# A five-layer graph network on one core: counts written tile by tile, x normalized by ScalarE, and the last neighbour sum with adjacency blocks stationary

## What is computed

```python
h = maximum(layernorm(x), 0)
# first network: encoder, five layers with shared GRU weights, decoder
h = maximum(h @ enc_w1.T + enc_b1, 0) @ enc_w2.T + enc_b2
for w in conv_w:                                  # 5 layers
    agg = segment_sum((h @ w)[src], dst)
    h = gru(agg, h)                               # gates r, z, n; wih, whh
h = maximum(h, 0)
x = x + sigmoid(maximum(h @ dec_w1.T + dec_b1, 0) @ dec_w2.T + dec_b2)
# second network: two sums with a normalized adjacency
h = maximum(layernorm(x), 0)
v = dinv[src] * dinv[dst]                         # dinv = degree ** -0.5, from src, loops added once more
h = relu(spmm(v, h) @ W1.T + b1)                  # 256 hidden features
x = x + spmm(v, h) @ W2.T + b2
```

## Time and profile before

| | before |
|---|---|
| median of 3 runs | 767.2 us (766.75 to 767.5) |
| the profiled execution | 767.26 us, span 765.5 us |
| mean granted clock of TensorE | 0.998 of full speed |
| busy TensorE / VectorE / ScalarE / GpSimd | 95% / 43% / 43% / 5% |
| chain that ended last | TensorE 83%, VectorE 10%, ScalarE 3% |

### The profile page before, as it was taken

The page is one execution under the profiler, slowest core; times in us unless marked ns, Lnnn a source line. Parts: engine busy times, 40 slices in busy tenths (PEclk is TensorE's granted clock), DMA queues, the critical chain, the costliest instruction groups (busy, mean ns, idle before and its releaser), DMA issues.

```text
span 765.5 us, 9328 instructions
## 1 busy us (share of the span) xinstructions
PE 726.1 (95%) x3792; PEld 370.4 (48%) x3792; DVE 331.5 (43%) x666; ACT 329.4 (43%) x452; POOL 40.2 (5%) x55
## 2 busy tenths in 40 slices
PE   2678999999999999999999999999999999999997
PEld 2545666544444445444454444544445545555443
DVE  7999998442412225122250322645654731123102
ACT  2687988653643336343363433523446411112000
POOL 5110000000000000000000000120000410000000
PEclk9999999999999999999999999999999999999999
DMA  6000020441501214013140032430001100000001
GB/s 181 5 1 2 1 73 2 77 96 37 97 0 36 48 36 88 1 21 62 36 88 1 14 69 37 79 93 2 1 0 64 39 1 1 2 1 2 23 20 46
DMA packets 78699, 28.38 MB, mean 37 GB/s; under 512 B 70245, under 2 KB 77798, under 8 KB 78523
## 3 DMA queue, kind: packets, MB, share of 16 engines
q1 hardware_dynamic: 77690, 26.93, 16.4%
q0 software_dynamic: 240, 0.66, 0.3%
q10 hardware_dynamic: 720, 0.13, 0.1%
HBM read 8.03 MB, written 2.60 MB: 14 GB/s over the span
## 4 chain that ended last, share of the span: by engine, by line
PE 83%; DVE 10%; ACT 3%; DMA 1%; issue 1%; POOL 1%; SPq 1%; DVEq 0%; ACTq 0%
PE PSA L1173 36%; PE PSA L1328 13%; PE PSA L1252 5%; DVE CT L816 4%; PE PSA L1185 3%; PE PSA L1194 3%; PE PSA L1187 3%; PE PSA L1189 3%; PE PSA L1193 3%; PE PSA L1196 3%; PE PSA L1116 3%; PE PSA L1316 2%; ACT AT L1486 1%; PE PSA L1304 1%; DVE stat L781 1%
## 5 line engine op out<-in xcount | busy, mean ns | idle before, releaser
L1173 PE MATMUL PSA<-AT,H 128*128 128x512 fp8e3 (+1 forms) x1522 | 287.0, 348 | 0.6 <-DMA H<-H 0.6
L1173 PEld LDWEIGHTS PSA<-AT,H 128*128 128x128 f16 x1522 | 131.6, 98 | 158.2 <-issue 13.6
L1009 DVE SCALAR_TENSOR_TENSOR rS<-PSA,bias,rS 128x512 f32<-128x512 f32 (+1 forms) x35 | 23.9, 682 | 270.6 <-ACT rS L1537 270.6
L1537 ACT ACTIVATE rS<-PSA,bias 128x512 f32<-128x512 f32 (+1 forms) x35 | 22.1, 632 | 203.7 <-PE PSA L1193 203.7
L1486 ACT ACTIVATE AT<-PSA 128x1000 fp8e3<-128x1000 f32 (+1 forms) x79 | 92.0, 1231 | 25.1 <-PE PSA L1116 24.8
L816 DVE TENSOR_TENSOR CT<-CT 128x2048 bf16<-128x2048 bf16 x80 | 92.2, 1204 | 3.0 <-PE PSA L1116 3.0
L1460 ACT ACTIVATE CTL<-AT 128x3125 fp8e3<-128x3125 fp8e3 (+1 forms) x25 | 69.9, 2797 | 0.0
L1116 PE MATMUL PSA<-CT 128*128 128x125 bf16 x625 | 48.5, 232 | 20.5 <-DVE CT L816 16.9
L1328 PE MATMUL PSA<-CT,H 128*128 128x512 fp8e3 (+1 forms) x336 | 65.5, 351 | 1.2 <-POOL H L726 1.2
L1328 PE MATMUL PSA<-CT,AT 128*128 128x512 fp8e3 (+1 forms) x336 | 65.0, 351 | 0.0
L1116 PEld LDWEIGHTS PSA<-CT 128*128 128x128 bf16 x625 | 42.2, 103 | 34.3 <-DVE CT L816 24.0
(11 more groups left out here) (166 smaller groups left out, 644.8 us busy)
## 6 DMA issues: line engine op xcount, KB each, us to landing
AT<-scale_scratch SPq DMA_DIRECT2D x1, 1562.5 KB, 6.4
H<-in_x SPq DMA_DIRECT2D x1, 1536.0 KB
out<-AT SPq DMA_DIRECT2D x6, 256.0 KB
comb_scratch<-CT SPq DMA_DIRECT2D x1, 960.0 KB, 4.2
comb<-comb_scratch SPq DMA_DIRECT2D x5, 192.0 KB, 3.1
H<-yS SPq DMA_TRANSPOSE x48, 2.5
H<-in_x SPq DMA_DIRECT2D x1, 512.0 KB, 5.0
CT<-AT SPq DMA_TRANSPOSE x25, 3.9
```

The source lines that it names most:

```text
L1173: last = nc.tensor.matmul(bank[:, 0:w], H16[:, l % 2, t, h, :], AT3[:, t, n0:n0 + w], start=(t == 0 and h == 0), stop=(t == T - 1 and (h = ...
```

## The change

Three parts.

First, ScalarE's eviction of a group of counts goes over tiles outside and windows inside: for each tile it writes 8 x 5 = 40 neighbouring bytes, and reads five counts from each of eight windows. Before, it went over windows outside: for each window and tile it wrote 5 bytes.

Second, VectorE no longer normalizes: it computes -mean x scale for a chunk (`shifts`, one instruction of four elements), and ScalarE does `Relu(scale * x + shift)` tile by tile, after the evictions of an odd batch. VectorE's eviction of the transposed chunk becomes a plain copy.

Third, in the second sum the block of counts from 128 sources to 128 destinations is stationary, and the two halves of Z16 of that source tile, 256 columns, move. A tile u of 128 destinations is a chain of 24 such matmuls and one of 128 columns with ZP (`tile_sum`, `tile_ends`), and its bank has nodes on partitions, the high halves' sum in columns 0 to 127 and the low halves' in 128 to 255. No transposes follow: VectorE adds the two halves, scaled, to x in two chained instructions. Five banks (TILES) rotate. The last two tiles (53 nodes) are summed and turned as before. SP stores two tiles at a time.

```diff
-        SUM1, SUM2 = (1, 0, 6), (0, 7, 1)
+        SUM1, TILES = (1, 0, 6), (0, 7, 4, 1, 6)
+        STARTED = len(TILES)
@@ SyncE
-            for c in range(NC):
-                sp.wait_ge(output_ready, c + 1)
...
+            for g in range(FG):
+                if g == FG // 2:
+                    sp.wait_ge(last_output_ready, 1)
+                    for (p0, p1), us, (n0, n1) in node_pairs(NC - 1):
+                        stored(p0, p1, us, n0, n1)
+                sp.wait_ge(output_ready, 2 * g + 2)
+                stored(0, P, (2 * g, 2 * g + 2), 2 * P * g, 2 * P * (g + 1))
@@ VectorE
-            def normalized(s):
+            def shifts(s):
 
                 t0, nt = CH[s]
                 dve.wait_ge(roots_ready, s + 1)
-                for t in range(t0, t0 + nt):
-                    k = rows(t)
-                    last = nc.vector.tensor_scalar(X32[0:k, t, :], X32[0:k, t, :], mv[0:k, t, 0:1], lnsc[0:k, t:t + 1],
-                                                   ALU.subtract, ALU.mult)
-                last.then_inc(tile_normalized, 1)
+                nc.vector.scalar_tensor_tensor(lnb[:, t0:t0 + nt], mv[:, t0:t0 + nt, 0], -1.0, lnsc[:, t0:t0 + nt],
+                                               ALU.mult, ALU.mult).then_inc(shifts_ready, 1)
...
-                nc.vector.tensor_scalar(aggS[:, 0:w], PS[EA][:, 0:w], 0.0, None, ALU.max).then_inc(x_copied, 1)
+                nc.vector.tensor_copy(aggS[:, 0:w], PS[EA][:, 0:w]).then_inc(x_copied, 1)
...
-                for c, (t0, nt) in enumerate(CU):
-                    dve.wait_ge(sum2_transposed, c + 1)
...
+                for u in range(2 * FG):
+                    bank = PS[TILES[u % STARTED]]
+                    dve.wait_ge(sum2_ready, u + 1)
+                    link(nc.vector.scalar_tensor_tensor(OUT[:, u, :], bank[:, 0:F], dinvO[:, u:u + 1], X32[:, u, :],
+                                                        ALU.mult, ALU.add))
+                    nc.vector.scalar_tensor_tensor(OUT[:, u, :], bank[:, F:2 * F], dinvO[:, u:u + 1], OUT[:, u, :],
+                                                   ALU.mult, ALU.add).then_inc(output_ready, 1)
@@ TensorE
+            def tile_sum(u, s0, s1):
+
+                for s in range(s0, s1):
+                    nc.tensor.matmul(PS[TILES[u % STARTED]][:, 0:2 * F], CT2[:, s // 2, nodes(u), s % 2],
+                                     Z16[:, s, :, :].rearrange("p h f -> p (h f)"), start=(s == 0), stop=False)
+
+            def tile_ends(u):
+
+                nc.tensor.matmul(PS[TILES[u % STARTED]][:, 0:F], CTL[:, nodes(u)], ZP[:, :], start=False, stop=True
+                                 ).then_inc(sum2_ready, 1)
...
+            for u in range(STARTED, 2 * FG):
+                pe.wait_ge(output_ready, u - STARTED + 1)
+                tile_sum(u, 0, 24)
+                tile_ends(u)
@@ ScalarE
-                        AT3[0:P, :, w0 * W:(w0 + gw) * W].rearrange("p t (w d) -> p w t d", w=gw),
-                        counts[:, 0:gw, 0:W * T].rearrange("p w (t d) -> p w t d", t=T),
+                        AT3[0:P, :, w0 * W:(w0 + gw) * W].rearrange("p t (w d) -> p t w d", w=gw),
+                        counts[:, 0:gw, 0:W * T].rearrange("p w (t d) -> p t w d", t=T),
...
+            def normalized(s):
+
+                t0, nt = CH[s]
+                act.wait_ge(shifts_ready, s + 1)
+                for t in range(t0, t0 + nt):
+                    k = rows(t)
+                    last = nc.scalar.activation(X32[0:k, t, :], X32[0:k, t, :], ACT.Relu, bias=lnb[0:k, t:t + 1],
+                                                scale=lnsc[0:k, t:t + 1])
+                last.then_inc(tile_normalized, 1)
...
             for b in range(NBT):
                 windows(b)
+                if b % 2 == 1 and b // 2 < NC:
+                    normalized(b // 2)
```

More of the change, by code:

```diff
@@ L635, in _, with stored @@
             packed(ZP, Z16, projected_packed)
-            for c in range(NC):
-                sp.wait_ge(output_ready, c + 1)
[L638 to L645, removed]
+            def stored(p0, p1, u0, n0, n1):
+                r = u0[1] - u0[0]
+                sp.dma_start(out[n0:n1, :].rearrange("(i r) f -> i r f", r=r), OUT[p0:p1, u0[0]:u0[1], :]).then_inc(output_stored, 16)
+            for g in range(FG):
[5 more added lines that the diff above has]
+                stored(0, P, (2 * g, 2 * g + 2), 2 * P * g, 2 * P * (g + 1))
+            sp.wait_ge(output_stored, 16 * (FG + 2))
             sp.wait_ge(flag_ready, 1)
@@ L951, in biased_output @@
                     link(last)
+                    for u0, nu, k in [(0, 2 * FG, P)] + parts(NC - 1):
+                        last = nc.vector.tensor_scalar(dinvO[0:k, u0:u0 + nu], dinvU[0:k, u0:u0 + nu], 1.0 / S0, None, ALU.mult)
+                    link(last)
             def decoded_tail():
@@ L1393, in _ @@
             expand(NC - 1)
-            partial_sum(SUM2[0], 0, Z16, 2, projected_lo)
+            tile_sum(2, 0, 16)
             project(NC - 2)
-            partial_sum(SUM2[0], 0, Z16, 3, projected_lo)
-            pe.wait_ge(dec2_biased, NC)
-            partial_sum(SUM2[1], 1, Z16, 0)
+            pe.wait_ge(sum1_scaled, NC)
+            tile_sum(3, 0, 16)
+            tile_sum(4, 0, 16)
             project(NC - 1)
-            for g in (1, 2, 3):
-                partial_sum(SUM2[1], 1, Z16, g)
@@ L1402, in _ @@
-            for g in (4, 5):
-                partial_sum(SUM2[0], 0, Z16, g, projected_lo)
-                partial_sum(SUM2[1], 1, Z16, g)
-            pe.wait_ge(sum1_scaled, NC)
-            partial_sum(SUM2[2], 2, Z16, 0)
-            partial_sum(SUM2[2], 2, Z16, 1)
+            pe.wait_ge(projected_lo, 5)
+            for u in range(STARTED):
+                tile_sum(u, 16, 20)
+            pe.wait_ge(projected_lo, 6)
+            for u in range(STARTED):
+                tile_sum(u, 20, 24)
@@ L1411, in _ @@
             pe.wait_ge(projected_packed, 64)
[L1412 to L1427 removed]
+            for u in range(STARTED):
+                tile_ends(u)
+            for u in range(STARTED, 2 * FG):
+                pe.wait_ge(output_ready, u - STARTED + 1)
+                tile_sum(u, 0, 24)
+                tile_ends(u)
+                if u == STARTED:
+                    n0, w = CH[NC - 1][0] * P, width(NC - 1)
+                    for s in range(0, 24):
+                        for h in range(2):
+                            nc.tensor.matmul(PS[ZB][:, 0:w], Z16[:, s, h, :], CT2[:, s // 2, n0:n0 + w, s % 2],
+                                             start=(s == 0 and h == 0), stop=False)
+                    nc.tensor.matmul(PS[ZB][:, 0:w], ZP[:, :], CTL[:, n0:n0 + w], start=False, stop=True).then_inc(last_summed, 1)
+                if u == STARTED + 1:
+                    pe.wait_ge(sum2_copied, 1)
+                    for j in range(2):
+                        last = nc.tensor.transpose(PS[IB][0:rows2(2 * FG + j), j * F:(j + 1) * F],
+                                                   aggS[:, nodes(2 * FG + j, FT * P)], ident[:, :])
+                    last.then_inc(sum2_transposed, 1)
             pe.wait_ge(flag_ready, 1)
```

66 lines of the change are left out of this document (20 added, 46 removed).

## The result

The changed kernel takes 761.97 us (median of 6, 761.14 to 763.26) against 767.27 us (6, 766.75 to 767.70): a ratio of 0.9933, with an interval from 0.9922 to 0.9944. The forecast was 760.6 us. The profiled execution takes 762.71 us with a span of 759.9.

The account below looks back on a forecast made before the run. VectorE's one-hots were taken to hold TensorE back before 66 us, with TensorE running without gaps after about 143 us. 767.3 less 4.5 (front) less 2.2 (last sum) gives 760.6 us, range 757.0 to 768.0.

Parts of the forecast that it names:

- 0.7 us for part 2 at the old price: Front: normalization moved to ScalarE, with evictions still at their old length, gains about 0.7 us.
- Evictions: ScalarE's count evictions, written tile by tile, go from 1.11 to 0.93 us from start to start.
- rivals 1 and 2: Count evictions: 1, unchanged, 764.4 us, chance 0.20; 2, slower through reads in runs of five, 769.2 to 772.5 us, chance 0.13.
- The front's term: Building of the counts, until about 143 us: moved normalization and quicker evictions together gain 4.5 us.
- the 0.3 us: Front after 66 us: of TensorE's 3.0 us of waits for evictions, quicker evictions take away 0.3 us.
- The 0.33 us for `shifts`: VectorE's new four-element instruction costs 0.33 us a chunk in place of 1.03, saving 0.70 us a chunk.
- Rival 4: Front: ScalarE's normalization is late each time, TensorE waits longer and the 4.5 us are lost; 765.1 us, chance 0.08.
- The matmuls of 256 columns: Last sum: each matmul with 256 moving columns takes 109.4 ns; the smaller matmuls cost 0.8 us in all.
- rival 3: Last sum: matmuls of 256 columns take 121.7 ns, costing 6.0 us; 766.6 us, chance 0.09.
- The last sum's 2.2 us: Second sum to the end: 2.2 us gained, from fewer transposes and a shorter end, less new waits and smaller matmuls.
- the 1.8 us of new waits: Last sum: TensorE newly waits 1.1 us for ZP and 0.7 us for the first output, 1.8 us in all.
- the end brings about 2: After the last eviction and around it: one small store last, in place of the tail's two, gains about 2 us.

Follow-up runs that it names:

- part 2 alone: Against the kernel before, only the normalization moved from VectorE to ScalarE, evictions and last sum as before: 767.94 us, ratio 1.0013.
- part 1 alone: Against the kernel before, only the evictions of counts go tile by tile, normalization and last sum as before: 765.05 us, ratio 0.9971.
- norm_even: Against the changed kernel, ScalarE's normalization moved one batch earlier, behind the encoder's evictions of the even batch: 759.12 us, ratio 0.9892.
- sum_alone: Against the kernel before, only the last sum changed, front and evictions as before: 766.72 us, ratio 0.9993.

## Why the prediction was right, and where not

**The bound was read rightly.** VectorE's waits before 66 us were what the front had to give, ScalarE the engine that would take over at the old price of an eviction: part 2 alone ran into it (4.8 us of waits for the relu), part 1 alone left VectorE's. The forecast said 0.7 us for part 2 at the old price. That its profiled execution is 0.69 us faster is partly luck: it won 1.19 at the gates and lost most of the rest before the last eviction, and its median won nothing.

**Evictions** were forecast at 0.93 us from start to start and came out at 0.89; rivals 1 and 2 fall with 1006 ns. Writing in longer runs and reading in shorter ones together save 0.24 us; no run changed one side alone, so that the broken write cost this much and the read costs nothing is argued, from an eviction that is no slower than the 1025 ns of the unbroken rows. The Trainium skill (Advanced Engine Details and Errata, PSUM Cachelines) says that an access in PSUM that isn't contiguous slows matmuls significantly; it speaks of TensorE. The prediction carried the penalty over to ScalarE's reads, and no such slowing shows here.

**The front's term was 1.5 us too small.** The step that failed is the 0.3 us that the prediction counted of the 3.0 us of waits for evictions after 66 us. It measured 1.9 us in the change and 2.3 us in part 1 alone, behind the fourteenth batch of windows. Up to that batch the change won 4.1 us where 4.2 were forecast, and there two errors cancel, which is luck. The 0.33 us for `shifts`, from L896 in the earlier trace rows, measured 0.07 us of VectorE's queue, so VectorE saves 0.96 us a chunk in place of 0.70, 5.8 us in six; and the waits for the relu, expected to take nothing from the sum, keep 1.7 of it back. `norm_even`, which has the same shifts and no such waits, wins 5.7 us there.

**Rival 4 was half true.** The normalization in front of the relu's eviction does make TensorE wait, 5.4 us in all, but VectorE's time and the quicker evictions gave more; moving it wins another 2.0 us at the gates. I had the place right, and its price at nothing was wrong.

**The matmuls of 256 columns** take 109.2 ns against 109.4, so rival 3 falls too: stationary columns four bytes apart cost nothing that shows under 256 moving ones.

**The last sum's 2.2 us didn't come.** The step that failed first is that the 1.8 us of new waits were counted as waits alone: in some executions the clock falls behind them, and the tile at 1.2 GHz costs 1.84 us more. The waits themselves came as counted: with them filled and the clock at 1.00, the stretch from the second sum to the last eviction's end takes 71.9 us, where 71.7 were forecast. The second is "the end brings about 2", 1.1 of it behind the last eviction: the two stores of the tail, with their 1.99 us of issue, were taken for what sets the end. Taking the general branch out of both kernels shows the passage over it to be 1.5 to 2.1 us of the end and most of that 1.99, and the stores' size and order to play no part that shows. Why the passage is 0.5 us dearer in the changed kernel stays open. The new sum alone doesn't make it so (5.93 us in `sum_alone`), and the fetches after the last store number two in the change and three before, so it isn't their count.

The profiled 762.71 is 2.1 us above 760.6 because these two (1.9 and 1.5) and 0.2 between the gates and the second sum outweigh the front's 1.5 us. That the median, 762.0, is nearer owes to executions like 761.2, in which the low clock is taken to be missing.

## What to carry to other kernels

Where two engines feed a third in turn, price both before and after, in every stretch where the third waits: at the gates either part alone bought 1.2 to 2.5 us, the two 5.7. In a loop written by hand, put work that no one waits for behind the instruction that someone waits for; the same four activations, moved behind the encoder's evictions, were worth 2 us. And when a rearrangement thins out the matrix engine for a moment, look at the granted clock in the tile after it, not only at the waits.

## What the runs showed of the hardware

- ScalarE's eviction of 1000 counts from fp32 to one byte lasts 1243 ns when it writes runs of 5 bytes and reads runs of 125 counts, and 1006 ns when it writes runs of 40 and reads runs of five.
- After two waits of 0.66 and 0.78 us with 0.6 us of small work between them, the granted clock fell to 0.50 for some three microseconds in three of five profiles that have these waits, and stayed at 1.00 in the other two.
- With a branch that is passed over at the end of five programs, the end takes 1.5 to 2.1 us more, and instruction fetches stand in the DMA view there; without it, none do after the last store.
- The same VectorE instruction of four elements a partition is 393 ns in one place and 160 ns in another.
